# One table store per tile, three skewed reads per head and score operands loaded a head ahead, in the attention loop of a three-layer network

## What is computed

```
Q, K, V = heads(x@Wq.T+bq), heads(x@Wk.T+bk), heads(x@Wv.T+bv)     # 16 heads of 16
scores = einsum('bhqd,bhkd->bhqk', Q, K) * scale
c2p = einsum('bhqd,shd->bhqs', Q, pos_key) * scale                 # s: 256 relative positions
c2p = take_along_axis(c2p, clip(k - q + 128, 0, 255))
p2c = einsum('bhkd,shd->bhks', K, pos_query) * scale
p2c = swapaxes(take_along_axis(p2c, clip(q - k + 128, 0, 255)))
ctx = softmax(scores + c2p + p2c) @ V
```

## Time and profile before

| what | value |
|---|---|
| median of 3 runs | 10873.97 us (10871.64 to 10885.4) |
| the profiled execution | 10901.8 us, its span 10900.0 us |
| attention loop in the profile | 664 to 4071 us from the span's start |
| TensorE, VectorE, ScalarE busy (span) | 8477.2, 8804.1, 5249.7 us |
| granted TensorE clock, mean | 0.908 of full speed |

### The profile page before, as it was taken

How to read it: one execution, slowest core, us unless ns; L and a number is a source line. 1 busy time by engine, 2 the same in 40 slices (tenths; PEclk the granted TensorE clock), 3 DMA queues, 4 the chain that set the end, 5 groups by cost and what they waited for, 6 DMA issues and landing times. The chain is left out here.

```text
span 10900.0 us, 175868 instructions
## 1 busy us (share of the span) xinstructions
PE 8477.2 (78%) x48140; PEld 4843.8 (44%) x48140; DVE 8804.1 (81%) x14209; ACT 5249.7 (48%) x8445; POOL 4802.1 (44%) x4272
## 2 busy tenths in 40 slices
PE   4569898899899884886777777776777777776688
PEld 1246666666666663553333323332333333332355
DVE  4558888888888876885998888888788888888788
ACT  1247777777777761112554444443454454544111
POOL 0000000000000000443888888887788888887344
PEclk7789999999999996998988888888998898888799
DMA  5578888888888883111111111111222112221111
GB/s 178 203 243 280 277 280 276 278 279 279 278 277 278 275 270 119 35 36 67 55 55 67 71 71 45 62 71 44 76 79 79 67 56 75 79 79 46 46 36 33
DMA packets 1218159, 1498.82 MB, mean 138 GB/s; under 512 B 101997, under 2 KB 1073277, under 8 KB 1185000
## 3 DMA queue, kind: packets, MB, share of 16 engines
q1 hardware_dynamic: 1217832, 1495.78, 42.0%
HBM read 932.33 MB, written 564.60 MB: 137 GB/s over the span
## 5 line engine op out<-in xcount | busy, mean ns | idle before, releaser
L2080 PE MATMUL mb_y_ps<-mb_g,ident 128*128 128x512 f32 x4096 | 2277.0, 670 | 750.6 <-DVE mb_g L1881 486.9
L1822 POOL TENSOR_TENSOR mb_bx<-mb_dtu,mb_bc 128x512 f32<-128x512 f32 x2048 | 2636.6, 1312 | 227.9 <-DVE mb_hs L1931 194.1
L2112 ACT ACTIVATE mb_dA<-mb_dt,mb_a_neg 128x512 f32<-128x512 f32 x2048 | 1407.5, 690 | 2417.0 <-DVE mb_hs L1931 1505.3
L1351 POOL MEMSET f_half<- 128x1 f32 x2 | 0.2, 100 | 3844.0 <-POOLq L124 3844.0
L2080 PEld LDWEIGHTS mb_y_ps<-mb_g,ident 128*128 128x128 f32 x4096 | 807.6, 211 | 1984.9 <-DVE mb_g L1881 780.4
L963 ACT ACTIVATE at_tab<-at_e_ps 128x384 f32<-128x384 f32 x2064 | 1013.5, 491 | 965.2 <-PE at_e_ps L880 964.5
L1017 DVE TENSOR_REDUCE at_nmax<-at_s_ps 128x1 f32<-128x1024 f32 x1025 | 1255.0, 1224 | 35.2
L896 PE MATMUL at_pT_ps<-ident,at_probs 128*128 128x128 f32 x8192 | 1111.8, 279 | 143.6 <-ACT at_probs L968 137.1
L968 ACT ACTIVATE at_probs<-at_s_ps,at_nmax 128x1024 f32<-128x1024 f32 x1025 | 1141.6, 1114 | 97.5 <-DVE at_nmax L1017 77.5
L1829 POOL TENSOR_TENSOR mb_g<-mb_hs_sb,mb_bc 128x512 f32<-128x512 f32 x704 | 901.1, 1280 | 452.7 <-DVE mb_hs_sb L1931 354.9
L896 PEld LDWEIGHTS at_pT_ps<-ident,at_probs 128*128 128x128 f32 x8192 | 917.0, 142 | 404.0 <-ACT at_probs L968 378.9
(11 more groups left out here) (227 smaller groups left out, 14386.3 us busy)
## 6 DMA issues: line engine op xcount, KB each, us to landing
at_tables<-at_tab SPq DMA_DIRECT2D x2064, 192.0 KB, 3.5
at_skew<-at_tables SPq DMA_DIRECT2D x1030, 256.0 KB, 3.1
mb_bc<-mb_bc_rows SPq DMA_DIRECT2D x256, 1024.0 KB, 6.6
at_skew<-at_tables SPq DMA_DIRECT2D x773, 128.0 KB, 3.4
at_opnd<-at_q_st SPq DMA_DIRECT2D x129, 210.0 KB, 3.4
at_opnd<-at_kl_st SPq DMA_DIRECT2D x129, 210.0 KB, 3.9
at_opnd<-at_kr_st SPq DMA_DIRECT2D x129, 210.0 KB, 5.1
at_eopnd<-at_q_st SPq DMA_DIRECT2D x130, 192.0 KB, 4.3
```

Of the source, the lines that this page charges most:

```text
L1822: pool.tensor_tensor(bx[:, s % RINGS, :], dtu[:, c, :], bc[:, 0, n, :], ALU.mult).then_inc(s_bx, 1)
L2080: nc.tensor.matmul(y_ps[:, c % 2, :], ident[:, :], g[:, s1 % RINGS, :], start=(n == 0), stop=(n == STATE - 1)).then_inc(s_y, 1)
L2112: nc.scalar.activation(dA[:, s % DA_RING, :], dt[:, c, :], ACT.Exp, scale=a_neg[:, c, n:n + 1]).then_inc(s_dA, 1)
```

## The change

The two stores of a tile become one DMA; three parts (tiles 0-2, 3-5, 6-7) replace four of two tiles; `eopnd` is gone, and the table products read rows 0 to 95 of `opnd`; the three loads of `opnd` for head n+2 are issued at tile 6 of head n, behind a wait for the scores of that head's last tile; each operand array has its own semaphores.

```diff
-    PARTS = tuple((t, t + 2) for t in range(0, TT, 2))
-    LAG = 3
+    PARTS = ((0, 3), (3, 6), (6, TT))
...
-            def store_table(n1, u1, e):
-                ge(sp, s_tab, n1 * NE + e + 1)
-                part = e // 2 // (TT // len(PARTS))
-                sp.dma_start(table_dram[u1, e % 2, e // 2, 0:P, SPAN:SPAN + BAND], tab[:, e, :]).then_inc(s_tw[part], 16)
+            def store_tables(n1, u1, t):
+                ge(sp, s_tab, n1 * NE + 2 * t + 2)
+                part = [t < z for _, z in PARTS].index(True)
+                sp.dma_start(table_dram[u1, :, t, 0:P, SPAN:SPAN + BAND].rearrange("s p u -> p s u"),
+                             tab[:, 2 * t:2 * t + 2, :]).then_inc(s_tw[part], 16)
...
                 n, u = h.n, h.u
                 ge(sp, s_add, n * TT)
                 ge(sp, s_S, n * TT)
-                load_opnd(n + 1, 1 - u)
-                ge(sp, s_E, (n + 1) * NE)
-                load_eopnd(n + 2, u)
                 for i in range(TT):
-                    for e in range(2 * i, 2 * i + 2):
-                        store_table(n + 1, 1 - u, e)
                     for part, (_, z) in enumerate(PARTS):
-                        if z - 1 + LAG - 1 == i + 1:
+                        if z + 1 == i:
                             load_skew(n + 1, 1 - u, part)
-                        if z - 1 + LAG - 1 == i + 1 + TT:
+                        if z + 1 == i + TT:
                             load_skew(n, u, part)
-                    if i == 0:
+                    if i == TT - 2:
+                        ge(sp, s_S, n * TT + TT)
+                        load_opnd(n + 2, u)
+                    store_tables(n + 1, 1 - u, i)
+                    if i == 2:
                         ge(sp, s_pv, n * TT)
                         load_val(n + 1, 1 - u)
...
                 if i == 0:
-                    ge(pe, s_op[u], h.j * 48 + 48)
+                    ge(pe, s_op[2][u], h.j * 16 + 16)
                     ge(pe, s_sk[0], h.n * 64 + 64)
...
-                if e == 0:
-                    ge(pe, s_eop[u1], h.j * 32 + 32)
+                if e < 2:
+                    ge(pe, s_op[e][u1], h.j * 16 + 16)
...
-                mm = nc.tensor.matmul(e_ps[:, 0:BAND], eopnd[:, u1, side, t * P:(t + 1) * P],
+                mm = nc.tensor.matmul(e_ps[:, 0:BAND], opnd[0:ROWS, u1, side, t * P:(t + 1) * P],
```

More of the change, by code:

```diff
@@ L725, in attention_loop @@
         opnd = sb("opnd", [OPND, 2, 3, T], BF16)
-        eopnd = sb("eopnd", [ROWS, 2, 2, T], BF16)
         tab = sb("tab", [P, NE, BAND])
@@ L740, in attention_loop @@
         c_ps = pb("c_ps", [P, BANK])
-        s_op = [sem(f"opnd_loaded{u}") for u in range(2)]
-        s_eop = [sem(f"eopnd_loaded{u}") for u in range(2)]
+        s_op = [[sem(f"{n}_loaded{u}") for u in range(2)] for n in ("q", "kl", "kr")]
         s_val = [sem(f"val_loaded{u}") for u in range(2)]
@@ L767, in load_opnd @@
                 for k, st in enumerate((q_st, kl_st, kr_st)):
[L768 to L772, removed]
+                    sp.dma_start(opnd[:, u, k, :],
+                                 st[bass.ds(n, 1), :, :].rearrange("a r t -> (a r) t")).then_inc(s_op[k][u], 16)
             def load_val(n, u):
@@ L776, in load_val @@
                              v_st[bass.ds(n, 1), :, :].rearrange("a p n -> (a p) n")).then_inc(s_val[u], 16)
-            def store_table(n1, u1, e):
-                ge(sp, s_tab, n1 * NE + e + 1)
-                part = e // 2 // (TT // len(PARTS))
-                sp.dma_start(table_dram[u1, e % 2, e // 2, 0:P, SPAN:SPAN + BAND], tab[:, e, :]).then_inc(s_tw[part], 16)
+            def store_tables(n1, u1, t):
[3 more added lines that the diff above has]
+                             tab[:, 2 * t:2 * t + 2, :]).then_inc(s_tw[part], 16)
             def load_skew(n1, u1, part):
                 a, z = PARTS[part]
-                ge(sp, s_tw[part], n1 * (16 * 2 * (z - a)) + 16 * 2 * (z - a))
+                ge(sp, s_tw[part], n1 * (16 * (z - a)) + 16 * (z - a))
                 for side, a1, z1, first, to, width in (
@@ L814, in head @@
                                      out[:, 1 - u, :]).then_inc(s_ctx[1 - u], 16)
-            load_eopnd(0, 0)
-            load_opnd(0, 0)
-            load_eopnd(1, 1)
+            for u in range(2):
+                load_opnd(u, u)
             load_val(0, 0)
-            for e in range(NE):
-                store_table(0, 0, e)
+            for t in range(TT):
+                store_tables(0, 0, t)
             for part in range(len(PARTS) - 1):
@@ L834, in _ @@
                 ge(sp, s_ctx[u], 16 * (heads // 2))
-            ge(sp, s_op[0], 48 * (heads // 2 + 1))
+            for k in range(3):
+                for u in range(2):
+                    ge(sp, s_op[k][u], 16 * (heads // 2 + 1))
             ge(sp, s_val[0], 16 * (heads // 2 + 1))
-            for u in range(2):
-                ge(sp, s_eop[u], 32 * (heads // 2 + 1))
+            for part, (a, z) in enumerate(PARTS):
+                ge(sp, s_tw[part], 16 * (z - a) * (heads + 1))
             for part in range(len(PARTS)):
@@ L960, in keep_table @@
                 part = [e < 2 * z for _, z in PARTS].index(True)
-                ge(act, s_tw[part], n1 * (16 * 2 * (PARTS[part][1] - PARTS[part][0])))
+                ge(act, s_tw[part], n1 * (16 * (PARTS[part][1] - PARTS[part][0])))
                 nc.scalar.activation(tab[:, e, :], e_ps[:, 0:BAND], ACT.Copy).then_inc(s_tab, 1)
```

## The result

The changed kernel takes 11032.43 us (median of 4 runs, 11025.58 to 11052.28); the kernel before took 10876.47 on the same chip (4 runs). The ratio is 1.0145 [1.0128, 1.0163]: slower by 156 us, outside the range of the prediction. The profiled execution of after took 11052.3 us, its span 11050.2.

A forecast was written before the change was run, and what follows sets the result against it. It took SP's full queue to make the read for `scores(5)` late. Turn 1 at 10.4 plus 16.0 gives 26.4 us a head against 26.62, 28 us less over 127 heads: 10,850 us, range 10,760 to 10,940.

The forecast's parts named there:

- SP is no longer full: SP's queue: 39 DMAs a head become 25, at most 21.3 us of 26 with three landing waits.
- The wait in `scores(5)` has no cause left: Ahead of turn 4: the last part's read is no longer late, at most 1.4 us a head comes back.
- A wait appears in `scores(2)`, ended by the read behind the operand loads: Ahead of turn 1: a wait of about 1.5 us a head for the read of tiles 3 to 5.
- the 2.2 at which the text called itself wrong: Sign of failure: the wait in `scores(2)` under 0.7 us or over 2.2.
- The new chain is 9.25 us from q to `scores(2)`: From q's issue through operand loads, store of tile 6 and middle read: old mean 9.35, less 0.1.
- q's excess: q landed in 3.5, 3.8 and 3.3 us against a least of 2.9; that excess was taken out, leaving 9.35.
- the growth of the read: Read behind tile 6, from 704 to 1152 KB: 459 KB at 366 GB/s, 1.25 us added to the chain.
- the two subtractions: Taken off the chain to `scores(2)`: q's landing time above 2.9 us, and `eopnd`, 393 KB at 291 GB/s, 1.35 us.
- `scores(2)` to turn 1 takes 0.95, turn 1 to turn 2 3.54: Steps of TensorE behind the wait in `scores(2)`, 0.95 and 3.54 us, taken from the trace of the kernel before.
- A rule against the row: Stores: by the skill's fixed 2.0 us a DMA, eight saved give up to 16 us a head; kept out of the sum.
- The rest, turn 2 to turn 6, 12.46 us: TensorE's steps between these turns, put at 3.15, 2.9, 3.0 and 3.41 us.
- Rival 2: Middle read comes later still, `scores(2)` at 10.25, a head 27.35 us: +0.73, +93 us, slower; chance 0.20.

The follow-up runs named there:

- one store alone: The kernel before with the two stores of a tile in one DMA and nothing else changed; 10877.09 us, 0.996 of the kernel before.
- no second copy: The kernel before, four parts and two stores a tile kept, with `eopnd` left out and the operand loads at tile 6; 10699.18 us, 0.9812.
- read first alone: The changed kernel with each part read ahead of the store of tile z, not behind it; 10919.56 us, 1.0013 of the kernel before.
- kr later: The changed kernel with kr's load moved behind the middle read, to tile 7; 10864.43 us, 0.9955 of the kernel before.
- the slowest kernel: The changed kernel with four parts of two tiles, each read ahead of the store of tile z, and kr loaded at tile 7; 11236.25 us, 1.0299.

## Why the prediction was wrong

Its picture held, its sizes did not. Point by point:

- *SP is no longer full.* Right. Its stores are issued 1.8 us after the turn, and it waits for ScalarE instead of landings. The estimate of 0.5 us for a combined store was 0.39 in the row shown. But the number of DMAs, to which the text put the late read of before, was not its main cause: with 31 DMAs a head (one store alone) the wait in `scores(5)` stayed, and with 37 (no second copy) it was gone.
- *The wait in `scores(5)` has no cause left.* Right; turn 3 to 4 is 2.94 us (2.9 forecast).
- *A wait appears in `scores(2)`, ended by the read behind the operand loads.* Right in place and releaser, wrong in size: 2.46 us where 1.5 was forecast, over the 2.2 at which the text called itself wrong. No table product waits for an operand load.
- *The new chain is 9.25 us from q to `scores(2)`.* This is the step that failed: it is 10.03 in the mean. Over all heads, from the issue of q to the last landing of the read, the chain is 9.97 us before and 9.97 after (`scores(2)` starts 0.06 behind it); a shortening by 0.1 and by the 0.64 of q's excess was forecast, and none came. The term that was mis-sized is the growth of the read, 459 KB at 366 GB/s, 1.25 us. The kernel without operand loads has such reads with no operand load ahead of them: from the first issue to the last landing the part of 704 KB takes 4.71 us, that of 1088 KB 6.17, that of 1152 KB 6.50 (means). So the 459 KB cost 1.79 us, 256 GB/s. The 366 came from one stretch of 2 us, in which 89% of the bytes moved were rows of reads. In after, from 2025 to 2029 us, they were 95%, and the engines moved 266 GB/s. One short stretch doesn't give the price. The medians of the DMAs of the kernel without operand loads, 1000 to 3000 us (KB each, us from issue to landing), say the same by the piece:

```profile
at_skew<-at_tables SPq DMA_DIRECT2D x312, 384.0 KB, 4.2
at_skew<-at_tables SPq DMA_DIRECT2D x234, 192.0 KB, 4.7
at_skew<-at_tables SPq DMA_DIRECT2D x158, 256.0 KB, 3.0
at_skew<-at_tables SPq DMA_DIRECT2D x157, 128.0 KB, 3.1
```

 A long read of three tiles lands 1.2 us later than one of two, a short one 1.6 later. 9.35 - 1.35 + 1.79 is 9.79, which covers 0.54 of the 0.78 that were missing. The other 0.24 stays open. If the 1.79 holds behind operand loads too, which no run shows, it lies in the two subtractions, q's excess and `eopnd`: q landed 0.75 us sooner than before (2.67 against 3.42 in the mean), as the text had reckoned (0.64), and not all of that reached the chain's end.
- *`scores(2)` to turn 1 takes 0.95, turn 1 to turn 2 3.54.* Wrong by 0.2 and 0.4 (1.14 and 3.95 in the mean): the second step that failed, a term put at nothing and not in the prediction at all as a mechanism, the clock. The prediction took what lies behind the wait from heads in which the wait was short enough for the clock to stay up.
- *A rule against the row* (up to 16 us a head for eight stores saved). It was rightly kept out of the sum: the eight stores alone gave 0.23 us a head. The fit that the prediction takes from the Trainium skill (DMA: Bandwidth & Descriptors, Anatomy of one DMA) is given there for DMAs that GpSimd issues; here the sync engine issues them.
- *The rest, turn 2 to turn 6, 12.46 us.* Right: 3.17 + 2.94 + 2.93 + 3.42 = 12.46.

The sum in a head: 26.4 forecast, + 0.75 for `scores(2)` (turn 6 + 10.20 against 9.45), + 0.19 from `scores(2)` to turn 1 and + 0.41 from turn 1 to turn 2, together 27.75, the measured mean over all heads. The eight needless matmuls confirm the last two as one term (0.60 here, 0.65 there).

Rival 2 was the right case (slower, by this very mechanism, decided from `scores(2)` at 9.67, where it came at about 10.2) and got 0.20. Its price of 27.35 a head lacked the clock, 0.6 us, and had 0.15 in turn 4 to 5 that didn't come; that its 10.25 is so near the measured 10.20 is in part luck, for it had the added bytes at 291 GB/s (1.58 us), not at the 256 measured. The text saw that its own value was 0.22 us from the point of decision, while it had taken 0.6 us out of the only examples there were. With these 0.6 us left in, the sum would have stood on the rival's side (10.05 against 9.67).

What the change does, by its parts: leaving out `eopnd` and moving the operand loads gives -1.9% (no second copy); the single store gives nothing there (1.0115 to 1.0145 with three parts, 0.9803 to 0.9812 with four) and -0.4% where SP is full; the cut into three parts costs 3.4 points. The version with four parts beats both kernels, 0.9803 [0.9787, 0.982].

What also stays open is the price of one transfer ahead of the read. 210 KB less gave 0.98 us, 384 KB less 0.77, 630 KB less 1.5; the 2.5 us windows of the earlier trace rows would give 0.74, 1.35 and 2.2. The DMA engines moved 277 GB/s over ten microseconds of the chain in after and 311 in the same ten before:

```profile
2020.00:2030.00 10.00, 7.71 (x91) 5.21 (x89) 8.01 (x12) 7.20 (x12) 0.00 (x0) 1.00 0.89 277
```

```profile
2025.20:2035.20 10.00, 8.18 (x96) 6.27 (x96) 8.04 (x13) 7.37 (x13) 0.00 (x0) 1.00 1.01 311
```

The first row is after, the second before. Over all heads the chain moved 323 GB/s before and 281 after. More of what is moved in after are the skewed reads, rows of 1024 bytes and less. By the times of the single packets (after, 1000 to 3000 us, all 16 engines) rows of 1536 bytes, the stores, move at 348 GB/s, rows of 1024 and 512 bytes, nearly all of them the reads, at 307 and 267. The Trainium skill (DMA: Bandwidth & Descriptors, How a descriptor splits into AXI transactions) says that a piece which doesn't start on a 256-byte boundary also fetches the bytes between the boundary below it and its start. Rows read with a step one element shorter mostly start off a boundary. That would make the reads slower than the stores, in the direction of these numbers; no run here tells it from other causes, the shorter rows for one, for none read the tables without the skew.

## What to carry to other kernels

Where a loop is held by a read that comes back through DRAM, look at the time from "stored" to "wanted" of each part, not at the number of DMAs: fewer, larger parts save issue time that may be no bound and lose time that is one. Price the growth of such a read from two reads of different size with the same things around them, and price what runs behind a longer wait at the lower clock as well. Count the reads that stand directly behind the store that they need, for the queue waits there: with three such reads a head the time moved by 1.05 us down (read first alone) and by 0.31 up (kr later, 26.18 to 26.49), with four the queue was late for all that follows (24.94 to 29.10, the kr load later too).

## What the runs showed of the hardware

- TensorE's granted clock was at 0.50 (1.2 GHz, of 2.4) behind an idle time of 2.62 us and at 1.00 again from 2061 on, 4 us later (windows of the result); behind the idle time of 2.18 us shown above it stayed at 1.00. It cost 0.65 us a head in the mean, as much as a fourth of the wait itself, and eight needless matmuls in the wait took it away. The Trainium skill (TensorE: Matmul & The Clock Gate, HAM oscillation) describes this pattern: a wait for a DMA in each round, behind which TensorE starts at half its clock. The trace agrees, in about every fourth head (34 of 127).
- One store of 384 KB took as long to issue as one of 192 KB (medians 0.36 and 0.37 us). Four reads behind three operand loads and a store took 2.64 us to issue in after, 0.66 each; with no load ahead of them 1.86 to 1.91 in the rows of the slowest kernel.
- A queue that waits for a store it has only just issued waited 3.77 us in the mean of 205 times (3.1 to 4.4 in nine of ten) in the kernel in which every read stood so. Its head was 29.10 us, that of four parts without it 24.94.
